# Second layer's expert tiles: gathered from one token table by a list, in place of rows sent into slots

## What is computed

```python
# second layer, experts: N = 16384 tokens, E = 8, K = 2, F = 512
C = math.ceil(1.25 * N / E)                       # 2560 places per expert
probs = softmax(xf @ gate_w.T); topk_vals, topk_idx = top_k(probs, 2)
pos = cumsum(onehot)[...] - 1                     # place within the expert
keep = pos < C
buf = zeros((E, C + 1, D)).at[flat_e, pos_safe].set(xf[token_ids])
h = gelu(einsum('ecd,edf->ecf', buf[:, :C], w1) + b1)
expert_out = einsum('ecf,efd->ecd', h, w2) + b2
out = sum over k of w[k] * expert_out[flat_e, pos]     # added to the token
```

## Time and profile before

| | us |
|---|---|
| median of three runs | 2234.13 (2231.75 to 2237.75) |
| the profiled execution | 2232.88 |
| its span | 2231.1 |
| busy: PE / DVE / ACT / POOL | 1648.6 / 1112.9 / 700.2 / 994.1 |
| mean share of the granted TensorE clock | 0.872 |

### The profile page before, as it was taken

The page is one execution under the profiler, slowest core; times in us unless marked ns, Lnnn a source line. Parts: engine busy times, 40 slices in busy tenths (PEclk is TensorE's granted clock), DMA queues, the critical chain, the costliest instruction groups (busy, mean ns, idle before and its releaser), DMA issues.

```text
span 2231.1 us, 35340 instructions
## 1 busy us (share of the span) xinstructions
PE 1648.6 (74%) x9963; PEld 1385.1 (62%) x9963; DVE 1112.9 (50%) x4216; ACT 700.2 (31%) x1435; POOL 994.1 (45%) x1025
## 2 busy tenths in 40 slices
PE   4999996999699999999999928850000039999954
PEld 4777775777598998988988728850000016666632
DVE  4465558555567544777678755693000002222248
ACT  0323232233154443555555420120000014444422
POOL 2000003453467777677544410037777745554520
PEclk9999998999899999999999969985555569999965
DMA  3164445643667966899698456401110012232258
GB/s 116 34 123 77 97 85 117 140 85 76 142 168 199 221 186 177 228 241 243 174 225 216 143 128 138 96 20 52 53 48 23 2 26 80 79 90 77 81 176 295
DMA packets 325472, 277.64 MB, mean 124 GB/s; under 512 B 72642, under 2 KB 301783, under 8 KB 325179
## 3 DMA queue, kind: packets, MB, share of 16 engines
q1 hardware_dynamic: 260026, 207.65, 38.8%
q0 software_dynamic: 31488, 55.94, 7.7%
q10 hardware_dynamic: 33792, 12.06, 2.0%
HBM read 167.37 MB, written 109.43 MB: 124 GB/s over the span
## 4 chain that ended last, share of the span: by engine, by line
PE 50%; issue 15%; DVE 13%; DMA 10%; POOL 6%; ACT 2%; DVEq 2%; SPq 1%; POOLq 0%
PE zp L714 9%; DMA slots_cap<-arena 7%; PE zp L1012 6%; PE tp L862 6%; POOL slots_cap L614 5%; PE tp L872 4%; PE tp L1025 3%; PE zp L884 3%; PE gp L884 3%; PE tp L794 2%; PE gp L809 2%; PE zp L872 2%; DMA arena<-slots 2%; PE gp L812 2%; DVE arena L1787 2%
## 5 line engine op out<-in xcount | busy, mean ns | idle before, releaser
L614 POOL DMA_INDIRECT slots<-arena x256 | 256.9, 1003 | 522.4 <-DVE arena L1553 376.9
L655 POOL DMA_INDIRECT results<-arena x304 | 303.1, 997 | 184.8 <-DVE arena L1629 118.3
L614 POOL DMA_INDIRECT slots_cap<-arena x256 | 254.0, 992 | 269.0 <-issue 226.6
L714 PE MATMUL zp<-arena 128*128 128x256 f32 x1024 | 242.1, 391 | 45.9 <-ACT arena L1071 45.6
L1005 PE MATMUL gp<-arena 128*128 128x128 f32 x160 | 26.6, 288 | 309.7 <-DVE arena L1787 309.7
L714 PEld LDWEIGHTS zp<-arena 128*128 128x128 f32 x1024 | 196.9, 196 | 76.1 <-ACT arena L1071 47.9
L677 POOL DMA_INDIRECT results<-arena x160 | 160.6, 1004 | 169.4 <-DVE arena L1802 130.7
L1005 PEld LDWEIGHTS gp<-arena 128*128 128x128 f32 x160 | 17.3, 142 | 343.3 <-issue 305.5
L862 PE MATMUL tp<-arena 128*128 128x256 f32 x912 | 222.1, 380 | 0.7 <-issue 0.7
L1629 DVE SCALAR_TENSOR_TENSOR arena<-tp,arena 128x256 f32<-128x256 f32 x304 | 134.6, 481 | 136.7 <-PE tp L872 107.6
L862 PEld LDWEIGHTS tp<-arena 128*128 128x128 f32 x912 | 161.8, 191 | 16.9 <-issue 1.1
(11 more groups left out here) (269 smaller groups left out, 3261.8 us busy)
## 6 DMA issues: line engine op xcount, KB each, us to landing
arena<-in_L_ffn_W SPq DMA_DIRECT2D x304, 192.0 KB
arena<-results SPq DMA_DIRECT2D x56, 512.0 KB, 5.2
arena<-slots SPq DMA_DIRECT2D x152, 134.0 KB
arena<-taps SPq DMA_DIRECT2D x64, 224.0 KB, 4.7
slots_cap<-arena SPq DMA_DIRECT2D x20, 536.0 KB
arena<-slots_cap SPq DMA_DIRECT2D x40, 268.0 KB, 2.9
arena<-in_x SPq DMA_DIRECT2D x8, 1024.0 KB, 8.6
arena<-arena SPq DMA_DIRECT2D x128, 64.0 KB
```

Source lines behind the costliest of these rows:

```text
L614: g.indirect_dma_start(slots[m], bass.IndirectOffsetOnAxis(ap=slot[:, k, blk:blk + 1].bitcast(U32), axis=0), rows[:, blk, :], None, bounds ...
L655: g.indirect_dma_start(results, bass.IndirectOffsetOnAxis(ap=row_at[:, q:q + 1].bitcast(U32), axis=0), y_tiles[:, q, :], None, bounds_chec ...
L714: t.matmul(dst, wg[:, j, k, :], xs[c][:, :, k, 0:P], start=(k == 0), stop=False)
```

## The change

- Slots, sends and fills of the second layer go. Tokens are stored once, in `table` (16384 rows of 134 words), four stores of 32 blocks, each when its norms are ready.
- The token number is now 128 * partition + block (before 128 * block + partition), so a partition's blocks lie together in `table` and in `results`. This changes the order of rows in `results` for the first layer too.
- DVE splits each slot into a tile (slot / 128) and a lane (slot mod 128). For each of the 256 pairs of block and choice, ACT writes a matrix `lanes` of signs (+1 where the wanted lane is at or past the column, else -1), DVE writes `tiles` (the value 2 * token + choice + 1 in the column of the tile, else 0), and PE adds their product to a 128x160 sum in PSUM. Neighbouring lanes of the sum differ by twice the value that belongs in the lane.
- DVE copies the sum, SP shifts it by one partition in two transfers between SBUF places, and DVE takes differences: `result_at` (result row of each place, or one out of bounds) and `token_at`.
- POOL gathers the rows of each tile from `table` by `token_at`, one indirect DMA per tile, up to three quads ahead, and still scatters the outputs. Its loop is written out. DVE no longer computes flags and result rows in the loop.

```diff
-        slots = [...] + [scratch("slots_cap", E8 * CAP, ROW_W)]
+        slots = [scratch(f"slots_{g}", G_PAIRS[g] * PAIR, ROW_W) for g in range(GROUPS)]
+        table = scratch("table", TOKENS, ROW_W)
...
-            by_token = results.rearrange("(k p s) c -> p k (s c)", p=P, s=2)
+            by_token = results.rearrange("(p k s) c -> p k (s c)", p=P, s=2)
...
-                    if c < 20:
-                        fill_slots(GROUPS, E8 * CT // 20 * c, E8 * CT // 20)
...
@@ SP, second layer
-            all_sent(GROUPS + 2)
+            for turn in range(NBLK // TURN4):
+                sp.wait_ge(sem("norm4_ready"), turn + 1)
+                part = slice(TURN4 * turn, TURN4 * turn + TURN4)
+                sp.dma_start(table.rearrange("(p k) w -> p k w", p=P)[:, part, :], rows[:, part, :]).then_inc(sem("table_out"), 16)
+            sp.wait_ge(sem("norm4_ready"), NBLK // TURN4 + 1)
+            sp.dma_start(at_lane[2][0:P - 1, :], at_lane[0][1:P, :]).then_inc(sem("table_out"), 16)
+            sp.dma_start(at_lane[2][P - 1:P, :], at_lane[1][0:1, :]).then_inc(sem("table_out"), 16)
...
-            load_quads(0, 0)
-            load_quads(0, 1)
...
@@ POOL
-            for r in (GROUPS, GROUPS + 1):
-                pool.wait_ge(sem("slots_ready"), r + 1)
-                for n in range(GB):
-                    for k in range(2):
-                        send(r, n, k)
...
+            def gather(Q):
+
+                m = Q % per
+                if Q >= per:
+                    pool.wait_ge(sem("quad_n_ready"), Q - per + 1)
+                for q in range(QT):
+                    tile = QT * Q + q
+                    g.indirect_dma_start(quad_in[m][:, q, :], None, table,
+                                         bass.IndirectOffsetOnAxis(ap=token_at[:, tile:tile + 1].bitcast(U32), axis=0),
+                                         bounds_check=TOKENS - 1, oob_is_err=False).then_inc(sem(f"quad_in{m}"), 16)
...
+            for Q in range(GATHERS_AHEAD):
+                gather(Q)
+            for Q in range(E8 * per):
+                if Q + GATHERS_AHEAD < E8 * per:
+                    gather(Q + GATHERS_AHEAD)
+                pool.wait_ge(sem("yq_ready"), Q + 1)
+                for q in range(QT):
+                    tile = QT * Q + q
+                    g.indirect_dma_start(results, bass.IndirectOffsetOnAxis(ap=result_at[:, tile:tile + 1].bitcast(U32), axis=0),
...
@@ PE
+            for n, (blk, k) in enumerate(HOTS):
+                pe.wait_ge(sem("lane_ready"), n + 1)
+                pe.wait_ge(sem("tile_ready"), n + 1)
+                t.matmul(inverse, lanes[n % ONE_HOT_RING], tiles[n % ONE_HOT_RING], start=(n == 0), stop=(n == len(HOTS) - 1)
+                         ).then_inc(sem("hot_done"), 1)
...
@@ ACT
+            for n, (blk, k) in enumerate(HOTS):
+                if n >= ONE_HOT_RING:
+                    act.wait_ge(sem("hot_done"), n - ONE_HOT_RING + 1)
+                A(lanes[n % ONE_HOT_RING], lane_no, ACT.Sign, bias=row_lane[:, k, blk:blk + 1], scale=-1.0
+                  ).then_inc(sem("lane_ready"), 1)
...
@@ DVE, router's part 7, for tile and lane
+                    o.step(v.tensor_scalar(tile.bitcast(I32), at, P.bit_length() - 1, None, ALU.arith_shift_right))
+                    o.link(v.tensor_scalar(lane.bitcast(I32), at, P - 1, None, ALU.bitwise_and))
+                    o.step(v.tensor_copy(tile, tile.bitcast(I32)))
+                    o.link(v.tensor_copy(lane, lane.bitcast(I32)))
+                    v.tensor_scalar(lane, lane, 0.5, None, ALU.add).then_inc(sem("slots_ready"), 1)
...
@@ DVE
+                v.tensor_scalar(tiles[n % ONE_HOT_RING], cap_tile, row_tile[:, k, blk:blk + 1], row_value[:, k, blk:blk + 1],
+                                ALU.is_equal, ALU.mult).then_inc(sem("tile_ready"), 1)
...
+            dve.wait_ge(sem("hot_done"), len(HOTS))
+            o.link(v.tensor_copy(here, inverse))
+            v.tensor_scalar(minus, inverse, -1.0, None, ALU.mult).then_inc(sem("norm4_ready"), 1)
+            dve.wait_ge(sem("table_out"), 16 * (NBLK // TURN4 + 2))
+            o.link(v.tensor_tensor(here, here, next_lane, ALU.subtract))
...
-                v.tensor_tensor(quad_second[:, m, :], quad_in[m][:, :, SLOT0], own[:, bass.ds(QT * Q, QT)], ALU.not_equal
-                                ).then_inc(sem("quad_flagged"), 1)
```

More of the change, by code:

```diff
@@ L125 @@
 TAIL = G_BLOCKS[2] // KB
-SENT = [2 * sum((G_BLOCKS + (GB, GB))[:n + 1]) for n in range(GROUPS + 2)]
+SENT = [2 * sum(G_BLOCKS[:n + 1]) for n in range(GROUPS)]
 F1 = 512
@@ L134 @@
 QT = 4
+ONE_HOT_RING = 8
+GATHERS_AHEAD = 3
 FIN_RING = 4
@@ L208, in metaformer @@
         row_id = arena.take(NBLK)
-        own = arena.take(E8 * CT)
+        own = arena.take(2 * max(G_PAIRS))
         fill = arena.take(ROW_W)
@@ L269, in metaformer @@
         conv_b = arena.take(P)
+        lane_no = arena.take(P)
+        cap_tile = arena.take(E8 * CT)
+        row_value = arena.take(2, NBLK)
+        row_lane, row_tile = arena.take(2, NBLK), arena.take(2, NBLK)
+        late = arena.take(1)
+        at_lane = [arena.take(E8 * CT) for _ in range(3)]
+        result_at, token_at = arena.take(E8 * CT), arena.take(E8 * CT)
         arena.at = front_end
@@ L286, in metaformer @@
         fb2 = [arena.take(P) for _ in range(2)]
+        quad_n = [arena.take(QT, P) for _ in range(2)]
+        arena.at = phase + 2 * CG * 12 * IMG
         quad_in = [arena.take(QT, ROW_W) for _ in range(CT // QT)]
-        quad_n = [arena.take(QT, P) for _ in range(2)]
-        quad_second = arena.take(CT // QT, QT)
-        quad_at = arena.take(CT // QT, QT)
+        quad_all = arena.tensor[0:P, phase + 2 * CG * 12 * IMG:arena.at]
+        assert arena.at <= front_end
+        lanes = [arena.take(P) for _ in range(ONE_HOT_RING)]
+        tiles = [arena.take(E8 * CT) for _ in range(ONE_HOT_RING)]
         quad_t = [arena.take(QT * P) for _ in range(2)]
@@ L335, in metaformer @@
                     for g in (1, 2) for n in range(G_BLOCKS[g - 1] // KC)}
+        inverse = gp[1][:, 0:E8 * CT]
+        HOTS = [(blk, k) for blk in range(NBLK) for k in range(2)]
         block = ctx.enter_context(nc.Block())
@@ L532, in _ @@
                     load_expert(2 * pair + s, s)
-                    load_quads(pair, s)
             for m in range(per):
@@ L662, in _ @@
                 g.memset(toep[n].rearrange("p a b c -> p (a b c)"), 0.0).then_inc(sem("toep_zero"), 1)
-            pool.wait_ge(sem("fill_out3"), 16 * 20)
-            for r in (GROUPS, GROUPS + 1):
-                pool.wait_ge(sem("slots_ready"), r + 1)
-                for n in range(GB):
-                    for k in range(2):
-                        send(r, n, k)
-            per = CT // QT
[L672 to L679, removed]
+            g.iota(lane_no, pattern=[[1, P]], base=0, channel_multiplier=0, **exact)
@@ new lines, in _ @@
+            g.iota(cap_tile, pattern=[[1, E8 * CT]], base=0, channel_multiplier=0, **exact)
+            for k in range(2):
+                g.iota(row_value[:, k, :], pattern=[[2, NBLK]], base=k + 1, channel_multiplier=2 * NBLK, **exact)
+            g.memset(late, 0.0).then_inc(sem("hot_const"), 1)
+            pool.wait_ge(sem("x2_ready"), CHUNKS + TAIL)
+            g.memset(quad_all, 0.0).then_inc(sem("hot_const"), 1)
+            pool.wait_ge(sem("hot_const"), 2)
+            per = CT // QT
@@ new lines, in _ @@
+            pool.wait_ge(sem("table_out"), 16 * (NBLK // TURN4))
+            pool.wait_ge(sem("norm4_ready"), NBLK // TURN4 + 2)
+            for Q in range(GATHERS_AHEAD):
[7 more added lines that the diff above has]
+                    g.indirect_dma_start(results, bass.IndirectOffsetOnAxis(ap=result_at[:, tile:tile + 1].bitcast(U32), axis=0),
+                                         y_quad[Q % 2][:, q, :], None, bounds_check=2 * TOKENS - 1, oob_is_err=False
+                                         ).then_inc(sem(f"yq_out{Q % per}"), 16)
@@ L1577, in route_part @@
                         o.link(v.tensor_tensor(weight[:, k, half], weight[:, k, half], pick, ALU.mult))
[L1578 to L1583, removed]
+                        o.link(v.tensor_copy(slot[:, k, half].bitcast(I32), best))
+                    at = slot[:, :, half].bitcast(I32)
+                    tile, lane = (z[:, :, half] for z in (row_tile, row_lane))
+                    o.step(v.tensor_scalar(tile.bitcast(I32), at, P.bit_length() - 1, None, ALU.arith_shift_right))
[3 more added lines that the diff above has]
+                    v.tensor_scalar(lane, lane, 0.5, None, ALU.add).then_inc(sem("slots_ready"), 1)
                 if part == 7:
@@ L1773, in _ @@
             route(GROUPS + 1)
+            dve.wait_ge(sem("hot_const"), 1)
+            for n, (blk, k) in enumerate(HOTS):
+                if n >= ONE_HOT_RING:
+                    dve.wait_ge(sem("hot_done"), n - ONE_HOT_RING + 1)
```

(16 more changed lines are left out.)

31 lines of the change are left out of this document (13 added, 18 removed).

## The result

The changed kernel takes 2170.1 us (median of five, 2161.2 to 2173.1) against 2234.1: ratio 0.9715, 95% interval 0.9696 to 0.9734, so 64 us or 2.9% faster. The forecast was 2155 in a range of 2122 to 2215. The profiled execution is the fastest of the five, 2161.2 us with a span of 2159.5. The median stands 9 us above the profiled execution; that this distance lies in the loop too is likely, but the median execution has no profile.

The account below looks back on a forecast made before the run. POOL's sends were taken to bound 1533 to 1817 us, TensorE the expert loop, then POOL. Products to 1619.2, first gather 1628.2, first scatter 1654.2, loop to 2069.5, plus 83.9 final stage and 1.8 gave 2155 us, range 2122 to 2215.

Parts of the forecast that it names:

- The count of DMAs: Second layer on POOL: 416 indirect DMAs become 320; 96 fewer at 1.297 us is 125 us.
- Router: Before the first product: five small DVE instructions more and one copy less in each of two routes, +2.0 us.
- Products: 256 sign-by-tile matmuls after the router: 0.32 us each plus 3 us cold start, 85 us; ends 74 and 149.
- I take 0.32: Pace in us of each of the 256 products, with three close engine paces and a pair of semaphores each.
- The rival of slow products: 256 products: a semaphore hop or the low clock stays, 0.5 us or more each; about 2201 us; chance 0.1.
- List: From the last product's sum to POOL's first gather: 9.0 us in total, 6.4 of it for the shift.
- the right end of my two: Lane shift between SBUF places: ends were a 3.0 us landing, or all 127 packets through one queue, 6.8 more.
- Loop: Expert loop: POOL's 8 DMAs per quad take 10.4 us; round trip level at 11.7; 0.3 stall for 36 quads, 11 us.
- the third rival: Expert loop: scatter Q waits for gather Q+2, PE's clock drops, 3.0 us more per quad, 2269 us; chance 0.08.
- the second: Rival in the expert loop: gathers land late, 4.5 us like the codebook's median; 2198 us; chance 0.12.
- In the last stage DVE covers them: Last stage: result loads in 4 KB runs, before 1 KB, counted as nothing; final stage unchanged at 84 us.
- They lie in a stage that PE fills, so I count nothing: First layer: removing the 20 fills of `slots_cap` from SP's queue counted as nothing (0 to 5 us gain).

Follow-up runs that it names:

- the old order: The changed kernel with the token numbering of before (128 x block + partition, 1 KB runs): 2165.1 us, ratio 0.9683.

## Why the prediction was right, and where not

- **The count of DMAs** (416 to 320, 1.297 us each) held: a gather has 1.00 us and a gap of 0.30. That gave the sign and most of the size. That the total came within 15 us is in part luck, since the errors of the first layer and of the last stage cancelled.
- **Router.** Five instructions, from 1515.64 to the first product's operand at 1516.70: 1.06 us, as taken. The whole step from the first layer's last loads to there was 2.4 us shorter than forecast; which part of it was is not traced. The table stores were hidden: POOL's first gather waited for DVE, not for them.
- **Products.** 76.5 us instead of 85. The pace was 0.29 us. DVE did not set it: its last tile block starts at 1590.9, ACT's last sign block at 1592.2 and the last product's second record at 1592.9. Between ACT and PE (busy 71.3 and 72.2 of 73 us) the trace does not decide. With PE at the low clock (granted 0.50 from 1517 to 1521) each took 0.53:

```profile
1520.31 0.36 DVE L1825 TENSOR_SCALAR arena<-arena 128x160 f32<-128x160 f32 x1 [0.17 <-PE gp L1070]
1520.84 0.36 DVE L1825 TENSOR_SCALAR arena<-arena 128x160 f32<-128x160 f32 x1 [0.17 <-PE gp L1070]
```

  "I take 0.32" for two semaphores each was too much: the engines were busy nearly all the time, so the semaphores cost next to nothing. The rival of slow products fell.
- **List.** 9.1 against 9.0; the shift took 5.95 us from issue, against 6.4. By the rule of the Trainium skill ("DMA: Bandwidth & Descriptors", the section on why a DMA increments its semaphore by 16) the whole 127 go through one engine; the cut into 112 and 15 agrees. So the right end of my two was the one queue, 9.8 us by 53 ns a packet, and that price was too high; the middle, 6.4, was near by luck.
- **Loop.** The step that failed is "11.7 us ... They are level ... I take 0.3". The chain was right in its members, and the trace of the change prices it (gather of quad 4 to scatter of quad 2):

```profile
1637.19 1.00 POOL L692 DMA_INDIRECT arena<-table,arena  x1 [0.30 <-issue]
...
1639.85 1.11 DVE L1850 TENSOR_SCALAR arena<-arena 128x128 f32<-128x128 f32 x4 [4.97 <-DMA arena<-table,arena]
1641.02 1.11 PE L1034 MATMUL gp<-arena 128*128 128x128 f32 x4 [5.15 <-DVE arena L1850]
...
1641.92 3.40 PE L1054 MATMUL tp<-arena 128*128 128x512 f32 x4
...
1648.93 0.69 DVE L1863 TENSOR_TENSOR arena<-zp,arena 128x512 f32<-128x512 f32 x1 [7.97 <-PE zp L1041]
...
1650.45 1.07 POOL L706 DMA_INDIRECT results<-arena  x1 [1.79 <-DVE arena L1863]
```

  The clock over these PE rows, and after them:

```profile
1641.02:1645.16 4.14, 4.14 (x8) 2.25 (x9) 0.00 (x0) 1.28 (x2) 3.12 (x4) 0.52 0.14 48
1645.16:1648.93 3.77, 3.77 (x34) 3.76 (x33) 0.00 (x0) 0.69 (x1) 2.90 (x3) 1.00 0.24 55
```

  13.3 us, not 11.7. Landing is 2.7. The extra lies in PE: 7.9 us from its start to the bias instead of 6.1, since after 5.15 us of idleness the transposes take 1.11 instead of 0.66 and the up products 3.40 instead of 1.88. This is the mechanism of the third rival at a fraction of its price. POOL waits in about every second quad (20 or 21 waits, 44 to 52 us in all, 5.1 of it ahead of the first scatter). The program's order says why: the gathers of Q+3 are issued before the wait of scatter Q, so what POOL waits there is slack for scatter Q+1. In the profile of the change 17 of the quads 1 to 36 have a wait, and none follows another. A longer trip therefore costs about half its excess per quad; both the second and the third rival counted it in full. The trips that end in one of these waits are 12.7 to 15.1 us long, 13.4 in the mean; six of the 17 exceed 13.8, the length at which the third rival put the break-even, and the program is still faster. Against the 10.47 us of the kernel with four quads ahead, the 36 intervals lose 28 us here and 40 in the profile of the old order, where 11 was forecast.
- **Last stage.** "In the last stage DVE covers them" failed. I asked only whether the loads would be late for DVE. They were not. ACT's waits for its own stores grew from 17.0 to 53.9 us, with two buffers for them, and the stage took 99.05 us instead of 83.8.
- **First layer.** "They lie in a stage that PE fills, so I count nothing" failed: one window of 30 us stood for 700, and the waits for tiles, which the view of waits shows as 42 us, were not counted. The stage ended 15.1 us earlier; with the fills back, 13.5 of them were gone.

## What to carry to other kernels

When an engine issues DMAs both for the start and for the end of a pipeline, write down the round trip and the engine's own work between the two, and give one more unit of lead than makes them level; here one constant was worth 43 us. A transfer that is hidden still takes part of the DMA engines: ask of each edit to it which other transfers it runs beside, and how many buffers those have. Removing background transfers can free a stage that looks full in one window; look at the waits over the whole stage first.

## What the runs showed of the hardware

- Loads in 4 KB runs instead of 1 KB, same bytes, beside stores of 256 KB with two in flight: the stores landed in 4.8 us instead of 3.6 (4.4 with 1 KB runs in the changed kernel), and the stage moved 254 instead of 300 GB/s. With four in flight they landed in 4.0 with 4 KB runs (302 GB/s) and 3.9 with 1 KB. Why the changed kernel with 1 KB runs and two buffers stood at 4.4 and not 3.6 stays open.
- After 5.15 us of idleness in the new loop PE ran 4.1 us at a granted clock of 0.52, then at 1.00; that lengthened a round trip, though PE was busy only 0.76 of the loop.
- Breaking the power-of-two step of 131072 bytes between partitions (132096 instead) gave no gain: ratio 0.9713 against 0.9715, last stage 102.5 against 99.05 us.
- A move within SBUF of 127 partitions x 640 bytes on SP's queue kept its reader waiting 2.6 us longer than the same move in 112 and 15.
